# Another order of the same operations in an attention and expert-FFN kernel: score tiles two to a slot in a head's first quarter, column maxima in the second, subtraction in the third, FFN slices last

## The reference

```python
for wl in range(16):                       # "wavelengths"
    m = cos(phase_modulators[wl])          # one number per head
    scores = einsum('bhqd,bhkd->bhqk', Q*m, K*m) / sqrt(8)
    scores = scores * cos(KERR * scores * scores)     # KERR = 2.7e-12
    acc += einsum('bhqk,bhkd->bhqd', softmax(scores), V) * interference_weights[wl]
x = layernorm(x + (acc / 16) @ Wo + bo)
probs = softmax(x @ router_w + router_b)   # 8 experts and a pass-through, top 2
y = sum_e gates[e] * (gelu(x @ w1[e]) @ w2[e]) + gates[8] * x      # F = 512
x = layernorm(x + y)
```

## Time and profile before

| | |
|---|---|
| time, median of 3 runs | 7853.22 us (7847.56 to 7853.93) |
| span of the profiled execution | 7846.0 us |
| ScalarE busy | 7197.4 us, 92% |
| VectorE busy | 6425.3 us, 82% |
| TensorE busy, matmuls | 6089.0 us, 78% |
| GpSimd busy | 30.2 us |
| DMA, mean over the span | 17 GB/s |
| exponentials on ScalarE (L484) | 6992.1 us busy, 446.8 us idle before them |
| value products (L550) | 31744 from the ring, 3959.7 us; 1024 from VectorE's part, 540.5 us |

### The profile page before, as it was taken

How to read it: one execution, slowest core, us unless ns; L and a number is a source line. 1 busy time by engine, 2 the same in 40 slices (tenths; PEclk the granted TensorE clock), 3 DMA queues, 4 the chain that set the end, 5 groups by cost and what they waited for, 6 DMA issues and landing times.

```text
span 7846.0 us, 120046 instructions
## 1 busy us (share of the span) xinstructions
PE 6089.0 (78%) x42436; PEld 2309.7 (29%) x42436; DVE 6425.3 (82%) x9807; ACT 7197.4 (92%) x2227; POOL 30.2 (0%) x108
## 2 busy tenths in 40 slices
PE   5777777777777777787877877877778777777777
PEld 2222222222232332332323323323233232332325
DVE  5888888888888888888888888888888888888873
ACT  3999999999999999999999999999999999999993
POOL 0000000000000000000000000000000000000000
PEclk8999999999999999898998989989899899999998
DMA  1000000000000000000000000000000000000000
GB/s 54 1 1 1 1 1 1 1 4 19 24 23 13 24 24 12 23 12 31 27 12 24 22 14 24 12 24 23 20 27 18 18 23 13 24 24 12 23 11 33
DMA packets 32188, 136.43 MB, mean 17 GB/s; under 512 B 3456, under 2 KB 21760, under 8 KB 25216
## 3 DMA queue, kind: packets, MB, share of 16 engines
q1 hardware_dynamic: 30848, 126.91, 4.4%
q0 software_dynamic: 768, 1.57, 0.1%
HBM read 117.98 MB, written 10.49 MB: 16 GB/s over the span
## 4 chain that ended last, share of the span: by engine, by line
DVE 33%; ACT 24%; issue 21%; PE 19%; ACTq 3%; DVEq 1%; DMA 0%; SPq 0%
ACT ring L484 23%; PE pv L550 11%; DVE km L681 7%; DVE vprobs L719 5%; DVE scores L696 5%; ACTq L479 2%; PE sc L515 2%; PE sc L532 2%; DVE vprobs L717 2%; DVE vrest L713 2%; DVE scores L675 1%; DVE numer L726 1%; DVE tile_h L771 1%; DVE vpower L712 1%; DVE vprobs L716 1%
## 5 line engine op out<-in xcount | busy, mean ns | idle before, releaser
L484 ACT ACTIVATE ring<-scores 128x4096 f32<-128x4096 f32 (+3 forms) x2048 | 6992.1, 3500 | 446.8 <-DVE scores L696 219.7
L550 PE MATMUL pv<-ring,vh 128*32 128x512 f32 x31744 | 3959.7, 628 | 1121.7 <-ACT ring L484 1031.9
L550 PEld LDWEIGHTS pv<-ring,vh 128*32 128x32 f32 x31744 | 991.9, 114 | 3709.6 <-issue 2233.7
L719 DVE SCALAR_TENSOR_TENSOR vprobs<-vprobs,vrest 128x512 f32<-128x512 f32 x1536 | 1062.9, 692 | 52.3
L515 PE MATMUL sc<-qt,km 128*128 128x512 f32 x2048 | 1009.5, 616 | 7.6 <-DVE km L671 7.6
L681 DVE TENSOR_REDUCE km<-scores 128x256 f32<-128x2048 f32 (+1 forms) x256 | 987.0, 3857 | 0.1
L675 DVE COPY scores<-sc 128x1024 f32<-128x1024 f32 (+1 forms) x512 | 624.0, 1219 | 220.5 <-PE sc L515 220.5
L696 DVE TENSOR_TENSOR scores<-scores,sc 128x1024 f32<-128x1024 f32 (+1 forms) x512 | 588.5, 1213 | 124.3 <-PE sc L532 124.3
L550 PE MATMUL pv<-vprobs,vh 128*32 128x512 f32 x1024 | 540.5, 610 | 125.7 <-DVE vprobs L720 125.7
L726 DVE COPY numer<-pv 128x512 f32<-128x512 f32 x512 | 350.2, 684 | 343.9 <-PE pv L550 339.5
L515 PEld LDWEIGHTS sc<-qt,km 128*128 128x128 f32 x2048 | 348.5, 189 | 627.4 <-issue 599.1
(11 more groups left out here) (153 smaller groups left out, 2682.9 us busy)
## 6 DMA issues: line engine op xcount, KB each, us to landing
tile_w<-in_L_ffn_w SPq DMA_DIRECT2D x48, 2048.0 KB, 7.8
ring<-in_L_ffn_w SPq DMA_DIRECT2D x2, 2048.0 KB, 11.4
scores<-in_L_attn_x SPq DMA_DIRECT2D x4, 512.0 KB, 4.2
qt_scratch<-qt SPq DMA_DIRECT2D x4, 512.0 KB, 2.6
kt_scratch<-kt_ SPq DMA_DIRECT2D x4, 512.0 KB, 2.6
v_scratch<-vv SPq DMA_DIRECT2D x4, 512.0 KB, 2.9
qt<-qt_scratch SPq DMA_DIRECT2D x4, 512.0 KB, 3.7
kt_<-kt_scratch SPq DMA_DIRECT2D x4, 512.0 KB, 4.5
```

What stands on the lines that cost most here:

```text
L484: nc.scalar.activation(ring[:, i % SLOTS, 0:cols], scores[:, bass.ds(n % 2, 1), half * CK:(half + 1) * CK, :].rearrange("p o k s -> p (o k ...
L550: last = nc.tensor.matmul(pv[g * VC:(g + 1) * VC, pair % 2, :], vh[:, buf, half * CK + k, :], probs, start=(half == 0 and k == 0), stop=(h ...
L719: then(nc.vector.scalar_tensor_tensor(probs, probs, coefficient, rest, ALU.add, ALU.mult))
```

## The change

The same instructions are issued in another order. In steps of a head (0 to 15), before and after:

| | before | after |
|---|---|---|
| score tiles, copies | one a step, 0 to 7 | two a step, 0 to 3 |
| column maxima | 8 to 11 | 4 to 7 |
| transposes of them, row maxima | 12 | 8 |
| broadcast | 13 | 9 |
| subtractions | four at 13, four at 14 | four at 9, four at 10 |
| keys masked for the head after | 14 | 15 |
| first FFN product in slices, copies | 8 to 11 | 11 to 14 |
| second FFN product | 8 to 11 | 11 to 14 |
| tile_finish | 11 | 14 |
| exponentials 1 to 7 on VectorE | 0, 1, 3, 5, 7 or 8, 9, 11 or 13 | 1, 3, 5, 7, 9, 11, 13 |

The waits for the slots of `sc` follow: the score tiles of steps 0 wait for the last readers of the slots in the head before, slices and second product for all subtractions.

```diff
-        def transpose_colmax(pe, m, tile_no=None):
+        def transpose_colmax(pe, m):
             pe.wait_ge(colmax_ready, m + 1)
-            if tile_no is not None:
-                pe.wait_ge(tile_hidden_copied, 4 * tile_no + 3)
+            pe.wait_ge(sc_free, SP_FREES * m + KT)
...
             if k == 0:
                 pe.wait_ge(tile_w1, 16 * (i + 1))
-                pe.wait_ge(sc_free, SP_FREES * m + KT)
+                pe.wait_ge(sc_free, SP_FREES * (m + 1))
+                pe.wait_ge(diff_ready, KT * (m + 1))
...
-                if nxt is not None:
-                    pe.wait_ge(sc_free, SP_FREES * nxt + KT)
-                else:
-                    pe.wait_ge(diff_ready, KT * NH)
+                pe.wait_ge(diff_ready, KT * (nxt + 1 if nxt is not None else NH))
...
+                    at = 4 * quad + wi
                     if nxt is not None:
-                        if quad < 2:
-                            score_tile(pe, nxt, 4 * quad + wi)
-                        elif quad == 3 and wi == 0:
-                            transpose_colmax(pe, nxt, tile_no if part == 1 else None)
-                        elif quad == 3 and wi == 1:
-                            broadcast_rowmax(pe, nxt, [None, (tile_hidden_copied, 4 * tile_no + 4), (tile_added, tile_no + 1)][part]
-                                             if tile_no is not None else None)
+                        if at == 0 and tile_no is not None:
+                            score_tile(pe, nxt, 0, slot_read=(tile_hidden_copied, 4 * tile_no + 3) if part == 2 else None)
+                            score_tile(pe, nxt, 1, slot_read=(tile_hidden_copied, 4 * tile_no + 4) if part == 2 else (tile_added, tile_no + START))
+                        elif at < 4:
+                            score_tile(pe, nxt, 2 * at)
+                            score_tile(pe, nxt, 2 * at + 1)
+                        elif at == 8:
+                            transpose_colmax(pe, nxt)
+                        elif at == 9:
+                            broadcast_rowmax(pe, nxt)
...
-                        elif quad == 2:
-                            tile_slice(pe, tile_no, nxt, wi)
-                    if tile_no is not None and part == 2 and quad == 2:
-                        tile_part_two(pe, tile_no, nxt, wi)
+                        elif 11 <= at < 15:
+                            tile_slice(pe, tile_no, nxt, at - 11)
+                    if tile_no is not None and part == 2 and 11 <= at < 15:
+                        tile_part_two(pe, tile_no, nxt, at - 11)
...
-            shares = {0: 1, 1: 2, 3: 3, 5: 4, 8 if part == 1 else 7: 5, 9: 6, 13 if part else 11: 7}
+            shares = {2 * p - 1: p for p in range(1, 8)}
...
+                    at = 4 * quad + wi
                     if nxt is not None:
-                        if quad < 2:
-                            copy_scores(dve, nxt, 4 * quad + wi)
-                        elif quad == 2:
-                            column_max(dve, nxt, wi)
-                        elif wi == 0:
+                        if at < 4:
+                            copy_scores(dve, nxt, 2 * at)
+                            copy_scores(dve, nxt, 2 * at + 1)
+                        elif at < 8:
+                            column_max(dve, nxt, at - 4)
+                        elif at == 8:
                             row_max(dve, nxt)
-                        elif wi < 3:
-                            for k in range(4 * (wi - 1), 4 * wi):
+                        elif at < 11:
+                            for k in range(4 * (at - 9), 4 * (at - 8)):
                                 subtract_max(dve, nxt, k)
-                            if wi == 2 and keys_for is not None:
-                                mask_keys(dve, keys_for)
                     if quad == 1 and wi and part == 1:
                         tile_part_one_vector(dve, i, wi - 1, then)
-                    if quad == 2 and part == 1:
-                        copy_hidden(dve, i, wi)
-                    if quad == 2 and wi == 3 and part == 2:
+                    if 11 <= at < 15 and part == 1:
+                        copy_hidden(dve, i, at - 11)
+                    if at == 14 and part == 2:
                         tile_finish(dve, i, then)
...
+                    if at == 15 and keys_for is not None:
+                        mask_keys(dve, keys_for)
```

More of the change, by code:

```diff
@@ L188, in pool_setup @@
                             tr_read, att_made, att_stored, gen_scores, gen_tr, ff_x1, ff_gelu, ff_expert,
-                            ff_added, ff_stored, tile_x1_made, tile_products, tile_out_free):
+                            ff_added, ff_stored, tile_x1_made, tile_products, tile_added, tile_out_free):
                 pool.sem_inc(started, START)
@@ L500, in scalar_main, with score_tile @@
                 quads(n + 1, 1, 4)
-        def score_tile(pe, m, k, first=False):
+        def score_tile(pe, m, k, first=False, slot_read=None):
             if k == 0:
@@ L512, in score_tile @@
                 pe.wait_ge(sc_free, SP_FREES * m + k - 1)
+            if slot_read is not None:
+                pe.wait_ge(*slot_read)
             for half in range(2):
@@ L524, in transpose_colmax, with broadcast_rowmax @@
             last.then_inc(sc_full, 1)
-        def broadcast_rowmax(pe, m, slot_read=None):
+        def broadcast_rowmax(pe, m):
             pe.wait_ge(sc_free, SP_FREES * (m + 1))
-            if slot_read is not None:
-                pe.wait_ge(*slot_read)
             for t in range(KT):
@@ L786, in tile_finish @@
                                            tile_z[:, :], ALU.mult, ALU.add).then_inc(tile_added, 1)
-            dve.wait_ge(tile_added, i + 1)
+            dve.wait_ge(tile_added, i + 1 + START)
             dve.wait_ge(tile_out_free, i + START)
@@ L825, in vector_head @@
                         tile_gates(dve, i, then)
-                    at = 4 * quad + wi
+                    if at == 15 and keys_for is not None:
+                        mask_keys(dve, keys_for)
                     if at in shares:
```

## The result

The changed kernel takes 8153.2 us (8151.8 to 8160.4) against 7851.5 (7847.6 to 7853.9) on the same chip: a ratio of 1.0387, interval 1.0373 to 1.0402. It is 301.7 us slower, where 172 was forecast. Its profiled span is 8150.2 us.

What follows compares the result with a forecast made beforehand. ScalarE's own work bounds the kernel, VectorE having little room. Pairs with a tile +5.4 us x 24 = +130, plain heads +40, end +2: 7853 + 172 = 8025, said as 8020 us; range 7835 to 8130, forecast's own 7940 to 8080.

Steps and rivals of the forecast that it cites:

- The clock doubles it: Rival, slower still: stalls leave TensorE at 1.2 GHz in two or three weighs a pair; 8140 us at most; chance 0.17.
- All eight subtractions end at step 10, so the two waits for L696 go: ScalarE's two waits for VectorE's subtractions vanish in pairs with a tile, winning 24 x some 6.5 = 160 us.
- TensorE's queue waits in it: Even head with a tile, second quarter: tile_transpose and router wait behind VectorE's column maxima; the head takes 18.3 us more.
- The tile steps don't hold TensorE: Rival, same time: layer norm and x1 copy come early enough, so only exponentials' due times count; 7842 us; chance 0.08.
- The early subtractions win: Rival, faster: ScalarE's four slots take in VectorE's second quarter; 7560 us, or 7682 for half of it; chance 0.15.
- Half clock, "I take 1.5": TensorE at half clock after its new stalls of 3 to 6 us adds 0 to 6 us a pair, 1.5 taken.
- VectorE's list: VectorE's in-order work from exponentials(2) to (4) in an even head with a tile: 34.4 us where ScalarE takes 27.2.
- Added 4, +3.1 for the odd head: Odd head with a tile: part two waits for the last subtraction, weigh 12 ends late; 115.0 + 3.1 = 118.2 us.
- Plain heads, "+40 us (32 to 47)": First 16 heads, without a tile: eight pairs lose about 5 us each from late weighs and exponentials, +40 us in all.
- 17.8 us of each pair is waiting, and four waits make it up: Kernel before, pairs with a tile: 241.8 us against ScalarE's floor of 224.0, the difference put down to four waits.
- "Costs nothing", GpSimd's store: GpSimd's store follows tile_finish by three steps, a pair's time before its buffer is wanted, so it costs nothing.
- "diff_ready, which slices and part two now wait for, is not free": FFN slices and part two wait for all subtractions; excluded from the free waits and counted within the heads with a tile.

Runs made afterwards that it cites:

- The shares alone: Kernel before with only VectorE's exponentials(p) moved to step 2p-1, all else as it was: 8072.4 us, ratio 1.0281.
- The edits of the slots, of GpSimd's queue and of the tile's steps with the logits: Changed kernel with fewer slot waits, GpSimd's value copies ahead of its store, and tile steps and logits earlier on VectorE, all together: 7860.3 us, 1.0013.
- the early shares: VectorE's exponentials 1 to 7 at steps 0, 1, 3, 5, 7, 9, 11: 8156.3 us in the changed kernel, 7819.7 us on top of the combined edits.
- One term less on VectorE: One polynomial term left out of VectorE's exponentials, nine instructions for ten: 7960.4 us in the changed kernel, 7696.7 us in the kernel before.

## Why the prediction was wrong

Slower was right, and so were the main places; the size was 130 us short and outside the range. The likeliest case wasn't the true one: "The clock doubles it", given 0.17 and 8140 at the most, comes closest. By steps:

*What stood.* "All eight subtractions end at step 10, so the two waits for L696 go": they went. "TensorE's queue waits in it" at `tile_transpose` and `tile_router`, forecast as 6 and 4 us, are 6.41 and 3.82, 24 times each. The waits for value products are 630.4 in the stage with tiles, over the 500 named. ScalarE waits at weighs 8 and 12 of the even head for 9.77 + 4.29 = 14.1 us, where 18.3 less the first quarter's 5.2 made 13.1. The loop edge still gives a half-clock weigh. *The tile steps don't hold TensorE* and *The early subtractions win* are refuted by these rows.

*Half clock, "I take 1.5": the term that failed.* The reason given, that "most of these stretches end behind VectorE's queue anyway", holds for weigh 8 (5.19, then 0.90 of waiting for the logits) and for the last two products of step 11 (1.89, then 2.55 of waiting for the subtractions). It doesn't hold for the two FFN products, behind which TensorE has its next work at once. By the rows, part two's first product and weigh 12 of the odd head cost 3.78 - 1.95 + 4.65 - 3.64 = 2.8 us, and the first slice and weigh 12 of the even head 3.78 - 2.05 + 4.21 - 3.64 = 2.3. That is 5.1 us a pair where 1.5 was taken, so 3.6 of the 5.2 us by which a pair was short. Weigh 0 is 6.49 in this pair (6.0 in the mean) for the 5.34 that was taken; ScalarE's waits in the first quarter, 4.95 + 0.50 + 0.50, are 0.8 over the 5.2 forecast, and the second quarter takes that up.

*VectorE's list* was also worked out too short, which makes up the rest. Counted as in the prediction, the last subtraction of the even head ends at 101.3 for 100.7 in this pair, and that of the odd head at 92.9 for 91.8; pair 14 of chunks (chunk 28) starts 2.9 us late in the even head (109.4 for 106.5), and in the odd one at 101.5, with weigh 12 forecast to end at 97.4. Late subtractions (0.6 and 1.1) and half clock (2.3 and 2.8) add up to that within 0.3 us. So *Added 4, +3.1 for the odd head*, is 0.29 + 2.11 + 4.25 = 6.65.

This split is worked out from rows. What a run shows is a part: three unused products at step 11 bring the first slice from 3.64 to 2.17 us in the mean, and the kernel wins 2.3 us a pair and 23 us in the plain heads. They cost something themselves (25 us in the order before), so what the clock costs in all may be more.

*Plain heads, "+40 us (32 to 47)"*, are +52.9, above that range. Its ends are the same sum with the last two products of step 11 at full clock (8 x 4.0) and at half clock (8 x 5.8). With the three products in the stall the plain heads lose 29.9, near the full-clock end. So the working of VectorE's queue seems right, and the clock behind the stall of step 11 mis-sized here too: 23 us for 15. That 29.9 comes so near to 32 may be in part luck: the unused products cost the plain heads 18 us in the order before, and in six of the kernels with the same plain heads head 16 starts anywhere from 1927.4 to 1941.5.

*The starting point.* "17.8 us of each pair is waiting, and four waits make it up" is a misreading: the four named are 3.87 + 3.12 + some 3 + 3.74 = 13.7. Two more stand between them, before chunk 4 of the odd head and before chunk 0 of the next, and make it some 17:

```profile
3940.32 13.71 ACT L484 ACTIVATE ring<-scores 128x4096 f32<-128x4096 f32 x4 [1.68 <-PE pv L550]
...
4043.72 7.12 ACT L484 ACTIVATE ring<-scores 128x4096 f32<-128x4096 f32 x2 [1.53 <-DVE scores L696]
```

*"Costs nothing", GpSimd's store.* I looked at the buffer's next use and not at what stands behind the store's wait. The copy of the values is late by it (a wait of 3.10 at weigh 0), a miss that the loop edge covers: 10 us in the run without it, about as much as the start of head 16 varies.

*"diff_ready, which slices and part two now wait for, is not free"*: it is the largest term that a single edit of the order gives back, 167 us when the wait is taken from the first slice and from part two, with the half clock behind it.

Not additive: the shares alone cost 221 us in the order before and win nothing back in the changed one, where no wait for the subtractions is left on ScalarE. The edits of the slots, of GpSimd's queue and of the tile's steps with the logits win 33 us more together than one by one, and behind them the early shares win 41, which alone won nothing. One term less on VectorE, finally, wins 6.6 us of a pair in both orders, so that gain doesn't explain the difference between them; that follows from the control alone and I would have had it wrong without it.

Left open: how the 10.6 us a pair split exactly between VectorE's lateness and the clock, since no run fills the odd head's FFN stall without holding TensorE elsewhere, and the 83 us for one step of exponentials(1) and (2).

## What to carry to other kernels

When an edit adds a stall of some us on TensorE, price the work behind the stall at the low clock unless a named later wait hides it; here that was, by rows, 3.6 of the 5.2 us by which a pair was short, and, as far as the run with three products shows it, a good part of the plain heads' error. Before moving work past an in-order engine's due times, list every input that another queue waits for, in order, since taking away the first wait may only show the second, as with the layer norm and the logits here. And run the same cut in the kernel before as a control: here it showed that a gain of 193 us in the changed kernel says nearly nothing of what the change brought, as the same cut wins 156 in the one before.

## What the hardware showed that was not expected

More clock isn't more speed: with seven unused products the mean granted clock rose from 0.89 to 0.922 and the kernel lost 30 us; with three it rose to 0.923 and it won 75. And the loop edge's idle of some 3 us doesn't by itself settle the clock of the weigh behind it. Of the seven edges in the plain heads with three fillers, four are at full speed behind 3.0 to 3.3 us of idle, and three take 5.3 behind 3.2 to 3.5; here is one of the four, and the edge at the same place in the changed kernel, in that order:

```profile
805.67 3.64 PE L554 MATMUL pv<-ring,vh 128*32 128x512 f32 x32 [3.34 <-issue]
```

```profile
813.05 5.29 PE L549 MATMUL pv<-ring,vh 128*32 128x512 f32 x32 [3.01 <-issue]
```

In the changed kernel itself one of the seven is at full speed, and in the kernel before none: all seven took 5.34. What decides it besides the idle time isn't shown; the only edit between the two kernels of these lines is the three products some steps before the edge.
